# A GRU scan on one core: one token block's input product moved between the one-product warm-up steps

## The chip, the cores and the metric

One core of one Trainium2 chip. The metric is the device time of one execution in microseconds (us); the kernel before took 2601.79 us in the median of three runs.

## What is computed

```python
def cell(h, x):                       # h [4, 1024], weights [1024, 3072]
    gi = x @ W_ih + b_ih
    gh = h @ W_hh + b_hh
    r = sigmoid(i_r + h_r); z = sigmoid(i_z + h_z)
    n = tanh(i_n + r * h_n)
    return (1 - z) * n + z * h
...
hs = scan(cell, cond, x over 1024 positions)      # x [4, 1024, 1024] f32
y = x + ffn(hs)    # layer norm, routing to one of 64 spline tiles, spline of 16 features
```

## The kernel before

**Work and layout.** The 4 sequences of 1024 positions are cut into 16 chunks of 64 positions, so 64 columns are scanned at once, in two sets (SETS) of 32. A chunk's start state isn't known, so the scan first warms up: from a zero state it runs the last 44 positions (20 to 63) of every chunk. 24 of these steps (WARM_HEADS) use one product, the f16 high part of the state by the high part of the weights; 20 (WARM_FULL) use three products (high by high, high by low, low by high). The end states become the next chunks' start states. Then the pass runs all 64 positions: 44 with three products, 20 as differences from sums stored in the warm-up. The pass also routes tokens, and a last part evaluates the splines. The one-product steps are called **heads** below, and one step of one set a half-step.

**Input product** (`input_product`, from L75). gi = x W_ih + b for all 4096 tokens in 8 blocks (NBLK) of 512 tokens, ordered by position, so block 0 holds positions 0 to 7 of all chunks and block 7 positions 56 to 63. A block is 24 PSUM banks (6 blocks of 512 weight columns, CBLOCKS, by 4 token tiles, TB). A bank takes 24 matmuls: 8 slices k of the inner dimension by three products of the split halves (L290 to L292). ACT makes the high halves (L184, L188), DVE the low ones (L229, L234). DVE evicts a bank, adding the bias (`evict`, L242), and ACT's queue stores it to `gi_scratch` in DRAM (`store_gi`). SP loads a block's x ahead (`load_x`, L126), the pieces of the weights (`load_w`, L123) and copies x rows (`begin_rows`, L131). In the last block W_hh is loaded and split into the room of W_ih, each column block after its last use.

**Recurrence** (`recurrence`, from L338). The split W_hh stays in SBUF. For a set, `pe_products` (L478 to L483) issues 8 x 4 matmuls of 512 columns into the set's r, z bank and 8 x 4 of 256 columns into its n bank; the four of a slice go to four column quarters of PE (128x32 weights). `dve_step` (L692) and `act_step` (L574) then run in turn: sums (L703, L706), sigmoids (L582, L583), r times n (L710), plus gi (L714), tanh (L587), new state (L719, L724), transpose (L728), and the f16 state for the next product (ACT, L592). PE, ACT and DVE each take set a, then set b, in the order of the code; sets alternate. In the heads the loop is

```python
with pe.Fori(0, WARM_HEADS // 2) as it:
    for u in range(2):
        pe_run(pe, it, u, 1, HEADS)
```

and alike on ACT and DVE. SP loads the gi record of a set two steps ahead: it waits until the slot's n part is used (`gi_used`, L1031) and issues four DMAs of 32 partitions by 3 KB (`load_gi`, L1024). These are 16 increments each on `gi_loaded`, for which DVE waits. Before the heads SP loads the spline tables and h0 (L1095, L1097), and POOL splits the tables. After the full steps SP issues, in this order, the records of the pass's first positions, the stores of sums and states, and the shifted start states (`shift_starts`, L1081), for which DVE waits before it sets the pass's start (L859). PE transposes routing hits between products in the pass (`pe_turn`, L521), and in the difference steps adds stored sums by 128x128 matmuls (L501) ahead of a product.

Of the kernel before, what the change touches and what calls it, by code (L numbers as in the profile page):

```python
# [73 lines left out]

def input_product(nc, ctx, t, W_ih, W_hh, b_ih, b_hh, xT, gi_dram, slopes, gamma, beta, gamma_t, beta_t,  # L75
                  out_scale, sign_dram, x_rows, hs_dram):
# [10 lines left out]
    x_hi = sb("x_hi", [P, 2, KB, BW], F16)  # L87
    x_lo = sb("x_lo", [P, 2, KB, BW], F16)
    out_stage = sb("out_stage", [P, TB, CW])
    bias_row = sb("bias_row", [P, QUARTERS, QW])  # L90
# [18 lines left out]
    sign_stored, rows_loaded, rows_ready = sem("sign_stored"), sem("rows_loaded"), sem("rows_ready")  # L109

# [4 lines left out]
    with nc.Block() as block:  # L115

        @block.sync
        def _(sp):
# [6 lines left out]
            def load_x(n, k):  # L125
                sp.dma_start(xstage[:, k:k + KX], xT.rearrange("(k p) n -> p k n", p=P)[:, k:k + KX, bass.ds(n * BW, BW)])\  # L126
                  .then_inc(x_loaded[k // KX], 16)
# [40 lines left out]
            with sp.Fori(1, NBLK - 1) as n:  # L168
                sp.wait_ge(x_hi_ready, n * XPARTS + XPARTS)
                sp.sem_inc(wait_carrier, 1)  # L170
                sp.wait_ge(x_lo_ready, n * XPARTS + XPARTS)
                sp.sem_inc(wait_carrier, 1)
                for k in range(0, KB, KX):
                    load_x(n + 1, k)
                begin_rows(n * 5 - 3, 5)

# [9 lines left out]
        def split_x_hi(act, n, buf, k):  # L186
            act.wait_ge(x_loaded[k // KX], n * 16 + 16)
            nc.scalar.activation(x_hi[:, buf, k:k + KX], xstage[:, k:k + KX], ACT.Copy, scale=S_SCALE).then_inc(x_hi_ready, 1)  # L188

        def store_gi(act, n, e):  # L190
            cb, tb = divmod(e, TB)
            act.wait_ge(acc_free, n * ACCS + (BANKS + e + 1))
            act.dma_start(gi_dram[bass.ds(n * BW + tb * P, P), cb * CW:(cb + 1) * CW], out_stage[:, tb]).then_inc(gi_stored[tb], 16)

        @block.scalar
        def _(act):
# [12 lines left out]
            with act.Fori(1, NBLK - 1, 2) as n:  # L209
                for u in range(2):  # L210
                    for e in range(ACCS):
                        if e == 8:
                            act.wait_ge(acc_ready, (n + u) * ACCS)
                            act.sem_inc(wait_carrier, 1)
                            for k in range(0, KB, KX):
                                split_x_hi(act, n + u + 1, u, k)
                        store_gi(act, n + u, e)
            for cb in range(CBLOCKS):
                for tb in range(TB):
                    store_gi(act, NBLK - 1, cb * TB + tb)  # L220
                act.wait_ge(acc_ready, (NBLK - 1) * ACCS + (cb + 1) * TB)
                for kp in range(XPARTS):
                    split_w_hi(act, PIECES + cb * XPARTS + kp, cb * XPARTS + kp)
            for b in range(TB):
                act.wait_ge(gi_stored[b], 16 * NBLK * CBLOCKS)
# [6 lines left out]
        def split_x_lo(dve, n, buf, k):  # L232
            dve.wait_ge(x_hi_ready, n * XPARTS + (k // KX + 1))
            nc.vector.scalar_tensor_tensor(out=x_lo[:, buf, k:k + KX], in0=xstage[:, k:k + KX], scalar=S_SCALE,  # L234
                                           in1=x_hi[:, buf, k:k + KX], op0=ALU.mult, op1=ALU.subtract).then_inc(x_lo_ready, 1)
# [11 lines left out]
        def _(dve):  # L247
# [19 lines left out]
            with dve.Fori(1, NBLK - 1, 2) as n:  # L267
                for u in range(2):
                    for e in range(ACCS):
                        if 12 <= e < 12 + XPARTS:  # L270
                            split_x_lo(dve, n + u + 1, u, (e - 12) * KX)
                        evict(dve, n + u, e, False)
            for cb in range(CBLOCKS):
                for tb in range(TB):
                    evict(dve, NBLK - 1, cb * TB + tb, False)
# [8 lines left out]
        def _(pe):  # L284
            def products(u, e, ks):
                cb, tb = divmod(e, TB)
                for k in ks:
                    hi, lo = x_hi[:, u, k, tb * P:(tb + 1) * P], x_lo[:, u, k, tb * P:(tb + 1) * P]
# [23 lines left out]
            with pe.Fori(1, NBLK - 1, 2) as n:  # L312
# [4 lines left out]
            pe.wait_ge(x_lo_ready, NBLK * XPARTS)  # L317
            for e in range(ACCS):
                whole(NBLK - 1, 1, e)
# [18 lines left out]
def recurrence(nc, ctx, t, h0, gi_dram, sums_dram, states_dram, hs_dram, x_rows, y_rows, tables):  # L338
# [16 lines left out]
    w_hi, w_lo, h, hi, flag = t["w_hi"], t["w_lo"], t["h"], t["hi"], t["flag"]  # L355
    lo = sb("lo", [P, SETS, JB, COLS], F16)
# [4 lines left out]
    saved = sb("saved", [P, SETS, 2, QW], F16)  # L361
# [11 lines left out]
    h_start = sb("h_start", [P, SETS, QF])  # L373
    next_start = sb("next_start", [P, SETS, QF])
# [8 lines left out]
    h_tok = sb("h_tok", [P, D])  # L383
    xhat = sb("xhat", [P, D])
    signed = sb("signed", [P, D])
    signs = sb("signs", [P, D], BF16)
# [4 lines left out]
    scores = sb("scores", [P, NT])  # L391
    tkeys = sb("tkeys", [P, NT])
    csums = sb("csums", [P, CLUSTERS])
    keys = sb("keys", [P, NT])
    best = sb("best", [P, 1])
    hit = sb("hit", [P, NT])
    hit_ids = sb("hit_ids", [P, NT])
    tile_id = sb("tile_id", [P, 1])
    row_f = sb("row_f", [P, 1])
    pick_now = sb("pick_now", [P, SLICE])  # L400
    row_now = sb("row_now", [P, 1], I32)
    affine_left = sb("affine_left", [NT, 2, 2 * SLICE])
    normal = sb("normal", [P, ENDS_MOST, SLICE])
    tok_ends = sb("tok_ends", [P, 2, ENDS_MOST])
    miss = sb("miss", [P, ENDS_MOST, NT])

    ends_hit = saved[:].rearrange("p s a f -> p (s a f)").bitcast(F32)[:, 0:ENDS_MOST * NT].rearrange("p (i t) -> p i t", t=NT)
    batch_ends = sb("batch_ends", [P, 2, NT])

    curves, *curves_left = (a[0:NT, 0:2 * SLICE * GRID] for a in (xhat, signed, h_tok))  # L410
    rstd, shift, hits, hits_t = t["rstd"], t["shift"], t["hits"], t["hits_t"]
# [5 lines left out]
    affine = pb("affine", [P, TILES, 2 * SLICE])  # L417

# [20 lines left out]
    wait_carrier = sem("wait_carrier2")  # L439
# [1001 lines left out]
```

## Time and profile before

| | |
|---|---|
| three runs | 2601.41, 2601.79, 2604.37 us |
| the profiled execution | 2604.53 us, span 2602.7 us |
| mean granted TensorE clock | 0.964 |
| input product, first to last matmul | 11.2 to 1019.2 us |
| heads, first matmul to first full step | 1032.20 to 1246.75 us |
| busy share of the span: PE, DVE, ACT, POOL | 90%, 50%, 26%, 7% |

The span is from the first to the last instruction; the execution's own time is 1.8 us more. Busy times are of one profiled execution. A matmul's record runs on while the next has begun, so a PE that is busy all the time isn't one at its peak; starts of successive matmuls tell the rate. The granted clock is a share of 2.4 GHz: 1.00 or 0.50 (1.2 GHz), in a stretch their mean.

### The profile page before, as it was taken

Reading aid. Unit: us, or ns where it says so; the run is one execution under the profiler, and the core shown is the slowest. Engines: PE = TensorE matmul, PEld = TensorE weight load, DVE = VectorE, ACT = ScalarE, POOL = GpSimd, SP = SyncE. Lnnn points to the kernel's source line nnn. Section 1 sums busy time; section 2 is a strip of 40 time slices with the busy share of each in tenths; the row PEclk is TensorE's granted clock in tenths of the full one; section 3 lists DMA queues with packets and bytes.
Section 4 is the critical chain, followed back from the end, with each engine's and each line's share of the span. In section 5 each row is a group of like instructions: output and inputs, shape, how many; then the busy total and the mean of one; then the engine's idle time right before and its main releaser. Section 6 shows DMA issues by size and latency. Waiting matters only on the chain. (4 is left out here: it accounts for less than half of the span.)

```text
span 2602.7 us, 83556 instructions
## 1 busy us (share of the span) xinstructions
PE 2354.0 (90%) x35300; PEld 1289.6 (50%) x35300; DVE 1291.3 (50%) x2644; ACT 668.9 (26%) x1340; POOL 189.1 (7%) x376
## 2 busy tenths in 40 slices
PE   7999999999999997666999998999999999977734
PEld 3444444444444443333666664666666666633311
DVE  4321121211111133777666664666666666877765
ACT  2200000000000012444333332333333333355520
POOL 0000000000000000000000000011111111121217
PEclk9999999999999998999999998999999999999955
DMA  6543131313131144333344443444444444477722
GB/s 213 182 150 125 53 121 54 121 53 122 51 140 53 49 150 141 95 88 87 120 138 129 136 138 86 122 114 113 114 120 122 113 114 120 122 225 222 221 50 4
DMA packets 160438, 305.21 MB, mean 117 GB/s; under 512 B 26832, under 2 KB 76416, under 8 KB 159296
## 3 DMA queue, kind: packets, MB, share of 16 engines
q1 hardware_dynamic: 122448, 236.06, 28.8%
q10 hardware_dynamic: 27648, 50.34, 5.2%
q0 software_dynamic: 10240, 17.31, 4.5%
q8 instruction: 80, 1.31, 0.2%
q14 instruction: 22, 0.18, 0.0%
HBM read 209.54 MB, written 144.18 MB: 136 GB/s over the span
## 5 line engine op out<-in xcount | busy, mean ns | idle before, releaser
L290 PE MATMUL acc<-w_hi,x_hi 128*128 128x512 f16 x1536 | 584.0, 380 | 19.7 <-DVE x_lo L234 11.2
L291 PE MATMUL acc<-w_hi,x_lo 128*128 128x512 f16 x1536 | 583.9, 380 | 0.0
L292 PE MATMUL acc<-w_lo,x_hi 128*128 128x512 f16 x1536 | 583.7, 380 | 0.0
L483 PE MATMUL rz_bank<-w_hi,hi 128*32 128x512 f16 x6912 | 427.7, 391 | 150.7 <-ACT hi L592 69.5
L242 DVE SCALAR_TENSOR_TENSOR out_stage<-acc,bias_row 128x512 f32<-128x512 f32 x192 | 132.3, 691 | 719.7 <-PE acc L292 719.7
L483 PEld LDWEIGHTS rz_bank<-w_hi,hi 128*32 128x32 f16 x6912 | 177.8, 98 | 326.9 <-ACT hi L592 81.5
L290 PEld LDWEIGHTS acc<-w_hi,x_hi 128*128 128x128 f16 x1536 | 150.6, 98 | 203.0 <-issue 16.0
L483 PE MATMUL rz_bank<-w_lo,hi 128*32 128x512 f16 x4096 | 243.1, 379 | 0.0
L483 PE MATMUL rz_bank<-w_hi,lo 128*32 128x512 f16 x4096 | 243.1, 379 | 0.0
L292 PEld LDWEIGHTS acc<-w_lo,x_hi 128*128 128x128 f16 x1536 | 150.6, 98 | 182.5 <-issue 2.2
L291 PEld LDWEIGHTS acc<-w_hi,x_lo 128*128 128x128 f16 x1536 | 150.6, 98 | 181.7 <-issue 1.7
L582 ACT ACTIVATE rz<-sums 128x512 f32<-128x512 f32 x176 | 110.9, 630 | 495.5 <-DVE sums L703 495.4
L483 PE MATMUL n_bank<-w_hi,hi 128*32 128x256 f16 x6912 | 232.9, 278 | 0.0
L703 DVE SCALAR_TENSOR_TENSOR sums<-rz_bank,gi 128x512 f32<-128x512 f32 x176 | 120.4, 684 | 205.2 <-PE rz_bank L483 204.6
L483 PEld LDWEIGHTS n_bank<-w_hi,hi 128*32 128x32 f16 x6912 | 189.7, 99 | 56.7 <-issue 6.8
L188 ACT ACTIVATE x_hi<-xstage 128x1024 f16<-128x1024 f32 x32 | 31.8, 1046 | 667.3 <-DVE out_stage L242 662.3
L483 PEld LDWEIGHTS rz_bank<-w_hi,lo 128*32 128x32 f16 x4096 | 109.0, 97 | 84.7
L483 PEld LDWEIGHTS rz_bank<-w_lo,hi 128*32 128x32 f16 x4096 | 109.0, 97 | 84.7 <-issue 0.2
L483 PE MATMUL n_bank<-w_hi,lo 128*32 128x256 f16 x4096 | 133.9, 273 | 0.0
L483 PE MATMUL n_bank<-w_lo,hi 128*32 128x256 f16 x4096 | 133.9, 273 | 0.0
L587 ACT ACTIVATE n_act<-n_sum 128x256 f32<-128x256 f32 x216 | 90.2, 418 | 166.6 <-DVE n_sum L714 166.0
L483 PEld LDWEIGHTS n_bank<-w_lo,hi 128*32 128x32 f16 x4096 | 109.0, 97 | 30.1
(158 smaller groups left out, 2013.8 us busy)
## 6 DMA issues: line engine op xcount, KB each, us to landing
gi<-gi_scratch SPq DMA_DIRECT2D x704, 96.0 KB
gi_scratch<-out_stage ACTq DMA_DIRECT2D x192, 256.0 KB, 2.1
gi<-sums_scratch SPq DMA_DIRECT2D x40, 512.0 KB
xstage<-in_xT SPq DMA_DIRECT2D x32, 512.0 KB, 6.0
y<-in_x_rows SPq DMA_DIRECT2D x32, 512.0 KB, 4.4
hs_scratch<-h SPq DMA_DIRECT2D x128, 128.0 KB
h_tok<-hs_scratch SPq DMA_DIRECT2D x32, 512.0 KB, 3.9
y<-hs_scratch POOLq DMA_DIRECT2D x32, 512.0 KB, 7.8
```

What stands on the lines that cost most here:

```text
L188: nc.scalar.activation(x_hi[:, buf, k:k + KX], xstage[:, k:k + KX], ACT.Copy, scale=S_SCALE).then_inc(x_hi_ready, 1)
L242: nc.vector.scalar_tensor_tensor(out=out_stage[:, tb], in0=acc[e % BANKS][:], scalar=UNSCALE, in1=bias_row[:].rearrange("p q f -> p (q f)" ...
L290: nc.tensor.matmul(acc[e % BANKS][:], hi, wh, start=k == 0, stop=False)
L291: nc.tensor.matmul(acc[e % BANKS][:], lo, wh, start=False, stop=False)
L292: last = nc.tensor.matmul(acc[e % BANKS][:], hi, wl, start=False, stop=k == KB - 1)
L483: last = nc.tensor.matmul(bank[q * COLS:(q + 1) * COLS, 0:b - a], state[:, s, j], w[:, j, q * QW + a:q * QW + b], start=first and j == 0, ...
L582: nc.scalar.activation(rz[:, s], sums[:, s, 0:RZ], ACT.Sigmoid).then_inc(rz_ready[s], 1)
L587: nc.scalar.activation(n_act[:, s], n_sum[:, s], ACT.Tanh).then_inc(n_ready[s], 1)
L703: nc.vector.scalar_tensor_tensor(out=sums[:, s, 0:RZ], in0=rz_bank[s][:], scalar=UNSCALE, in1=gi[:, s, u, 0:RZ], op0=ALU.mult, op1=ALU.add ...
```

## The change

- The input product makes blocks 1 to 7 only (EARLY_BLOCKS = 7). Block 0's x is loaded and split last, into `x_keep`, and is kept. After the first block's weight splits SP stores both halves of W_ih to DRAM (`late_w`, 16 DMAs).
- In the heads PE does 12 matmuls of 128x512 after each half-step's product (`pe_late`): slice k of one column block for the four token tiles, into the four PSUM banks that only later parts use. 48 half-steps are 6 column blocks by 8 slices. The weights come from `late_w` through a ring of four slots of 256 KB. After each eighth slice DVE evicts the four banks, two within its step and two behind it, and SP stores them to `gi_scratch`.
- A gi record is loaded by one DMA instead of four, in all stages that load them.
- The tables and h0 are loaded after the heads. PE and ACT wait after the heads for the last evictions, ACT before the pass for the row splits.
- Many tiles of the recurrence lie in the room of the kept x, the bias and the late results, with the same shapes.

The diff, cut to what the steps speak of:

```diff
             begin_rows(0, 2)
-            with sp.Fori(1, NBLK - 1) as n:
+            sp.wait_ge(w_hi_ready, PIECES)
+            sp.wait_ge(w_lo_ready, PIECES)
+            for k in range(KB):
+                for part, w in enumerate((w_hi, w_lo)):
+                    sp.dma_start(late_w[k, :, :, part],
+                                 w[:, k].rearrange("p (c f) -> p c f", f=CW)).then_inc(late_w_stored, 16)
+            with sp.Fori(1, EARLY_BLOCKS - 1) as n:
                 sp.wait_ge(x_hi_ready, n * XPARTS + XPARTS)
...
+                    evict(dve, EARLY_BLOCKS - 1, cb * TB + tb, False)
+                    if cb == 0:
+                        split_x_lo(dve, EARLY_BLOCKS, 1, tb * KX)
...
 
+        def pe_late(pe, cb, k):
+            pe.wait_ge(late_loaded[k % RING], cb * (KB // RING * 16) + (k // RING * 16 + 16))
+            pe.sem_inc(wait_carrier, 1)
+            wh, wl = late_ring[:, k % RING, 0], late_ring[:, k % RING, 1]
+            for tb in range(TB):
+                if k == 0:
+                    pe.wait_ge(late_free[tb], cb + 1)
+                    pe.sem_inc(wait_carrier, 1)
+                x_hi, x_lo = (x_late[:, part, k, tb * P:(tb + 1) * P] for part in range(2))
+                nc.tensor.matmul(late_acc[tb], x_hi, wh, start=k == 0, stop=False)
+                nc.tensor.matmul(late_acc[tb], x_lo, wh, start=False, stop=False)
+                last = nc.tensor.matmul(late_acc[tb], x_hi, wl, start=False, stop=k == KB - 1)
+                if k == KB - 1:
+                    last.then_inc(late_done, 1)
+            if k < KB - 1:
+                last.then_inc(late_used, 1)
         def pe_turn(pe, T):
...
             pe.sem_inc(hit_turned, 1)
-            with pe.Fori(0, WARM_HEADS // 2) as it:
-                for u in range(2):
-                    pe_run(pe, it, u, 1, HEADS)
+            def heads(cb):
+                for i in range(LATE_STEPS):
+                    pe_run(pe, cb * 2 + i // 2, i % 2, 1, HEADS,
+                           after=tuple((lambda k=i * SETS + s: pe_late(pe, cb, k)) for s in range(SETS)))
+            with pe.Fori(0, CBLOCKS) as cb:
+                heads(cb)
+            for tb in range(TB):
+                pe.wait_ge(late_free[tb], CBLOCKS + 1)
             with pe.Fori(WARM_HEADS // 2, WARM // 2) as it:
...
                 turns = p + 1
+                if first:
+                    act.wait_ge(rows_split, 5)
                 for s in range(SETS):
...
 
-        def dve_step(dve, it, u, s, seeds, mode=FULL):
+        def dve_late(dve, cb, tb):
+            dve.wait_ge(late_done, cb * TB + (tb + 1))
+            dve.sem_inc(wait_carrier, 1)
+            dve.wait_ge(late_stored[tb], cb * 16 + 16)
+            dve.sem_inc(wait_carrier, 1)
+            nc.vector.scalar_tensor_tensor(out=late_out[:, tb], in0=late_acc[tb], scalar=UNSCALE, in1=bias_room[:, bass.ds(cb * CW, CW)],
+                                           op0=ALU.mult, op1=ALU.add).then_inc(late_free[tb], 1)
+        def dve_step(dve, it, u, s, seeds, mode=FULL, after_sums=None, after_old=None):
             n = steps_to(it, u)
...
                                                op0=ALU.mult, op1=ALU.add).then_inc(hn_ready[s], 1)
+                if after_sums:
+                    after_sums()
                 dve.wait_ge(rz_ready[s], n)
...
             nc.vector.tensor_tensor(z_old[:, s], rz[:, s, QF:RZ], h_old, ALU.mult).then_inc(z_old_ready[s], 1)
+            if after_old:
+                after_old()
...
                     dve.sem_inc(h_stored[s][u], 16)
-            with dve.Fori(0, WARM_HEADS // 2) as it:
-                for u in range(2):
+            for tb in range(TB):
+                dve.sem_inc(late_free[tb], 1)
+                dve.sem_inc(late_stored[tb], 16)
+            with dve.Fori(0, CBLOCKS) as cb:
+                for i in range(LATE_STEPS):
                     for s in range(SETS):
-                        dve_step(dve, it, u, s, 1, HEADS)
+                        if i * SETS + s < KB - 1:
+                            dve_step(dve, cb * 2 + i // 2, i % 2, s, 1, HEADS)
+                        else:
+                            dve_step(dve, cb * 2 + i // 2, i % 2, s, 1, HEADS, lambda: dve_late(dve, cb, 0), lambda: dve_late(dve, cb, 1))
+                            dve_late(dve, cb, 2)
+                            dve_late(dve, cb, 3)
             for s in range(SETS):
...
 
-        def gi_rows(pos, s, q, a, b):
-            return gi_dram[bass.ds(pos * POS + s * COLS, COLS), q * QW + a:q * QW + b]
+        def load_late(sp, cb, k):
+            sp.dma_start(late_ring[:, k % RING], late_w[k, :, bass.ds(cb, 1)].rearrange("p o a f -> p (o a) f"))\
+              .then_inc(late_loaded[k % RING], 16)
 
         def load_gi(sp, pos, s, u):
-            for q in range(QUARTERS):
-                sp.dma_start(gi[q * COLS:(q + 1) * COLS, s, u, 0:QW], gi_rows(pos, s, q, 0, QW)).then_inc(gi_loaded[s][u], 16)
+            sp.dma_start(gi[:, s, u, 0:QW], gi_dram[bass.ds(pos * POS + s * COLS, COLS)].rearrange("c (q f) -> q c f", q=QUARTERS))\
+              .then_inc(gi_loaded[s][u], 64)
 
...
                     load_gi(sp, LEN - WARM + u, s, u)
+            for k in range(RING):
+                load_late(sp, 0, k)
+            def heads(cb, last):
+                for i in range(LATE_STEPS):
+                    for s in range(SETS):
+                        it, u, k = cb * 2 + i // 2, i % 2, i * SETS + s
+                        gi_used(sp, it, s, u)
+                        load_gi(sp, it * 2 + (LEN - WARM + 2 + u), s, u)
+                        if k < KB - RING or not last:
+                            if k < KB - 1:
+                                sp.wait_ge(late_used, cb * (KB - 1) + (k + 1))
+                            else:
+                                sp.wait_ge(late_done, cb * TB + TB)
+                            sp.sem_inc(wait_carrier, 1)
+                            load_late(sp, cb + (k + RING) // KB, (k + RING) % KB)
+                for tb in range(TB):
+                    sp.wait_ge(late_free[tb], cb + 2)
+                    sp.sem_inc(wait_carrier, 1)
+                    sp.dma_start(gi_dram[tb * P:(tb + 1) * P, bass.ds(cb * CW, CW)], late_out[:, tb]).then_inc(late_stored[tb], 16)
+            with sp.Fori(0, CBLOCKS - 1) as cb:
+                heads(cb, False)
+            heads(CBLOCKS - 1, True)
             sp.dma_start(curves, tables[:]).then_inc(curves_loaded, 16)
             for q in range(QUARTERS):
                 sp.dma_start(next_start[q * COLS:q * COLS + BATCH, 0], h0[q]).then_inc(h0_loaded, 16)
-            with sp.Fori(0, WARM_HEADS // 2) as it:
-                for u in range(2):
-                    for s in range(SETS):
-                        gi_used(sp, it, s, u)
-                        load_gi(sp, it * 2 + (LEN - WARM + 2 + u), s, u)
             for s in range(SETS):
...
             def one_pass(p, first):
+                if first:
+                    for tb in range(TB):
+                        sp.wait_ge(late_stored[tb], (CBLOCKS + 1) * 16)
                 for u in range(2):
```

## Rows read from the trace of the kernel before

**Rows 1.** The page: busy time of the whole span, and one matmul group.

```profile
PE 2354.0 (90%) x35300; PEld 1289.6 (50%) x35300; DVE 1291.3 (50%) x2644; ACT 668.9 (26%) x1340; POOL 189.1 (7%) x376
...
L290 PE MATMUL acc<-w_hi,x_hi 128*128 128x512 f16 x1536 | 584.0, 380 | 19.7 <-DVE x_lo L234 11.2
```

**Rows 2.** Busy time by stretch; columns: stretch, then length and busy us (x instructions).

```profile
500.00:550.00 50.00, 50.00 (x234) 22.63 (x232) 6.23 (x9) 0.00 (x0) 0.00 (x0) 1.00 0.14 53
1100.00:1150.00 50.00, 31.22 (x716) 18.14 (x720) 38.38 (x90) 24.11 (x49) 0.00 (x0) 1.00 0.32 90
1300.00:1350.00 50.00, 50.00 (x1237) 32.85 (x1228) 31.44 (x65) 17.88 (x39) 0.00 (x0) 1.00 0.44 142
```

**Rows 3.** Timeline of DVE and PE in one half-step of the heads.

```profile
1099.77 0.65 DVE L703 SCALAR_TENSOR_TENSOR sums<-rz_bank,gi 128x512 f32<-128x512 f32 x1
...
1103.91 0.65 DVE L703 SCALAR_TENSOR_TENSOR sums<-rz_bank,gi 128x512 f32<-128x512 f32 x1
...
1104.49 0.40 PE L483 MATMUL rz_bank<-w_hi,hi 128*32 128x512 f16 x4 [1.36 <-ACT hi L592]
```

**Rows 4.** Timeline of PE: first product of the heads, first product of the full steps.

```profile
1032.20 3.60 PE L483 MATMUL rz_bank<-w_hi,hi 128*32 128x512 f16 x32 [12.99 <-ACTq L636]
...
1246.75 1.91 PE L483 MATMUL rz_bank<-w_hi,hi 128*32 128x512 f16 x32 [1.36 <-ACT hi L592]
```

**Rows 5.** Busy time by stretch: start of the heads, and a later 5 us.

```profile
1035.00:1040.00 5.00, 5.00 (x104) 3.08 (x96) 2.73 (x6) 1.35 (x3) 0.00 (x0) 0.73 0.58 171
...
1150.00:1155.00 5.00, 5.00 (x88) 2.75 (x80) 4.01 (x10) 2.21 (x6) 0.00 (x0) 0.66 0.31 83
```

**Rows 6.** Timeline of DVE, last bank evictions of block 0; start us, duration us.

```profile
141.52 0.69 DVE L242 SCALAR_TENSOR_TENSOR out_stage<-acc,bias_row 128x512 f32<-128x512 f32 x1 [3.36 <-PE acc L292]
...
146.70 0.69 DVE L242 SCALAR_TENSOR_TENSOR out_stage<-acc,bias_row 128x512 f32<-128x512 f32 x1 [3.36 <-PE acc L292]
```

**Rows 7.** Timeline of PE in a full step.

```profile
1582.84 1.89 PE L483 MATMUL rz_bank<-w_hi,hi 128*32 128x512 f16 x32
1584.57 1.04 PE L483 MATMUL n_bank<-w_hi,hi 128*32 128x256 f16 x32
1585.44 1.89 PE L483 MATMUL rz_bank<-w_lo,hi 128*32 128x512 f16 x32
```

**Rows 8.** Timeline of PE where column quarters meet a wider tile.

```profile
1730.88 1.05 PE L483 MATMUL n_bank<-w_hi,lo 128*32 128x256 f16 x32
1731.86 0.30 PE L521 MATMUL hit_bank<-ident,hit 128*64 128x128 f32 x1
1732.08 1.91 PE L483 MATMUL rz_bank<-w_hi,hi 128*32 128x512 f16 x32
...
2358.01 1.05 PE L483 MATMUL n_bank<-w_hi,hi 128*32 128x256 f16 x32
2358.99 0.60 PE L501 MATMUL rz_bank<-gi,ident_sum 128*128 128x512 f16 x2
```

**Rows 9.** The page's DMA queues: packets, MB, share of 16 engines' span.

```profile
q1 hardware_dynamic: 122448, 236.06, 28.8%
```

**Rows 10.** Timeline of SP's DMA issues and of DVE at the pass's start.

```profile
1093.97 14.23 SPq L1024 DMA_DIRECT2D gi<-gi_scratch  x16
...
1564.78 1.76 SPq L1024 DMA_DIRECT2D gi<-gi_scratch  x4
...
1567.13 3.38 SPq L1081 DMA_DIRECT2D next_start<-h  x4
...
1571.84 0.29 DVE L859 COPY h_start<-next_start 128x256 f32<-128x256 f32 x1 [7.47 <-DMA next_start<-h]
...
2356.09 0.36 SPq L1049 DMA_DIRECT2D gi<-sums_scratch  x1
```

**Rows 11.** SP's issue of block 2's x; an issue group (KB each, us to landing).

```profile
143.60 2.09 SPq L126 DMA_DIRECT2D xstage<-in_xT  x4
...
hs_scratch<-in_x_rows SPq DMA_DIRECT2D x6, 2560.0 KB, 14.3
```

More of the change, by code:

```diff
@@ L86, in input_product @@
     xstage = sb("xstage", [P, KB, BW])
-    x_hi = sb("x_hi", [P, 2, KB, BW], F16)
-    x_lo = sb("x_lo", [P, 2, KB, BW], F16)
+    x_even = sb("x_even", [P, 2, KB, BW], F16)
+    x_hi, x_lo = ([x_even[:, part], t["x_keep"][:, part]] for part in range(2))
     out_stage = sb("out_stage", [P, TB, CW])
-    bias_row = sb("bias_row", [P, QUARTERS, QW])
+    bias_row = t["bias_row"]
     bias_h = sb("bias_h", [P, QUARTERS, RZ])
@@ L175, in _ @@
                 begin_rows(n * 5 - 3, 5)
+            sp.wait_ge(x_hi_ready, EARLY_BLOCKS * XPARTS)
+            sp.wait_ge(x_lo_ready, EARLY_BLOCKS * XPARTS)
+            for k in range(0, KB, KX):
+                load_x(EARLY_BLOCKS, k)
+            begin_rows(27, 5)
             for m in range(PIECES):
@@ L208, in _, with act_block @@
                 store_gi(act, 0, e)
-            with act.Fori(1, NBLK - 1, 2) as n:
-                for u in range(2):
[L211 to L217, printed above, removed]
+            def act_block(n, buf):
+                for e in range(ACCS):
+                    if e == 8:
+                        act.wait_ge(acc_ready, n * ACCS)
+                        act.sem_inc(wait_carrier, 1)
+                        for k in range(0, KB, KX):
+                            split_x_hi(act, n + 1, buf, k)
+                    store_gi(act, n, e)
+            with act.Fori(1, EARLY_BLOCKS - 2, 2) as n:
+                for u in range(2):
+                    act_block(n + u, u)
+            act_block(EARLY_BLOCKS - 2, 0)
+            act.wait_ge(acc_ready, (EARLY_BLOCKS - 1) * ACCS)
+            for k in range(0, KB, KX):
+                split_x_hi(act, EARLY_BLOCKS, 1, k)
+            act.wait_ge(late_w_stored, 16 * 2 * KB)
             for cb in range(CBLOCKS):
                 for tb in range(TB):
-                    store_gi(act, NBLK - 1, cb * TB + tb)
-                act.wait_ge(acc_ready, (NBLK - 1) * ACCS + (cb + 1) * TB)
+                    store_gi(act, EARLY_BLOCKS - 1, cb * TB + tb)
+                act.wait_ge(acc_ready, (EARLY_BLOCKS - 1) * ACCS + (cb + 1) * TB)
                 for kp in range(XPARTS):
@@ L311, in _ @@
                 whole(0, 0, e)
[L312 removed]
+            with pe.Fori(1, EARLY_BLOCKS - 2, 2) as n:
                 for u in range(2):
@@ L316, in _ @@
                         whole(n + u, 1 - u, e)
-            pe.wait_ge(x_lo_ready, NBLK * XPARTS)
-            for e in range(ACCS):
-                whole(NBLK - 1, 1, e)
+            for u in range(2):
+                pe.wait_ge(x_lo_ready, (EARLY_BLOCKS - 1 + u) * XPARTS)
+                for e in range(ACCS):
+                    whole(EARLY_BLOCKS - 2 + u, 1 - u, e)
 TILE_UNIT, CLUSTER_UNIT = 64, 272
@@ L439, in recurrence @@
     wait_carrier = sem("wait_carrier2")
+    late_loaded = [sem(f"late_loaded{i}") for i in range(RING)]
+    late_free, late_stored = ([sem(f"{n}{i}") for i in range(TB)] for n in ("late_free", "late_stored"))
+    late_used, late_done = sem("late_used"), sem("late_done")
     row_known, hit_kept, picked, pick_kept = (sem(n) for n in ("row_known", "hit_kept", "picked", "pick_kept"))
@@ L1113, in one_pass @@
             def one_pass(p, first):
+                if first:
+                    for tb in range(TB):
+                        sp.wait_ge(late_stored[tb], (CBLOCKS + 1) * 16)
                 for u in range(2):
```

101 lines of the change are left out of this document (58 added, 43 removed).

## The prediction

> **What bounds the kernel now.** I read the page first: PE is busy 90% of the span [rows 1]. That share mixes stages, so the next view was busy time by stretch [rows 2]. In the input product (500 to 550 us) PE is busy the whole time, DVE 6.2 us and the DMA engines 14%: PE alone sets the time. In the warm-up steps of one product (1100 to 1150 us; called heads below) PE is busy 31.2 of 50 us, DVE 38.4 and the DMA share is 0.32. In the full steps (1300 to 1350 us) PE is full again. So work in the first stage costs its whole PE time, and the heads have PE time to spare: the change carries work from the one to the other.
>
> The timeline of the heads says what they wait for [rows 3]. A half-step (one step of one set) is 32 matmuls of 512 columns and 32 of 256, four at a time on column quarters. DVE begins the sums of one set at 1099.77 and of the other at 1103.91: 4.14 us a half-step. From the sums to the first matmul that uses their state is 1104.49 - 1099.77 = 4.72 us, all of it DVE and ACT in turn. DVE works through one set's chain, waits for ACT included, before it takes the other's, so DVE's order bounds this stage. 48 half-steps at 4.14 us are 198.7 us, yet the stage runs from 1032.20 to 1246.75 [rows 4], 214.55 us; part of the rest is short spells at TensorE's lower level, such as a mean granted clock of 0.66 at 1150 to 1155 us [rows 5].
>
> **What is removed.** One of eight token blocks leaves the input product. A bank is evicted each 146.70 - 141.52 = 5.18 us [rows 6], which is 24 matmuls of 0.216 us; a block is 24 banks: **-124.3 us**, all of it on the path that sets the end.
>
> **What the heads get.** Each half-step gets 12 matmuls of the same shape: 12 x 0.216 = 2.59 us. Its own product, when nothing is waited for, takes 1585.44 - 1582.84 = 2.60 us [rows 7]. Together 5.19 us, over DVE's 4.14, so PE becomes the bound. Does the chain hide? From the start of a set's product its sums begin at most 2.6 us later, when the whole product is done, and the state is back 4.72 us after that: 7.3 us. The set's turn on PE comes again after two half-steps, 10.4 us or more. It hides with 3 us to spare. In every eighth half-step DVE also evicts four banks at 0.69 us [rows 6], 2.8 us; the spare 1 us of each half-step takes it back within three, and PE uses the four banks again only after the next product, 2.6 us on. I cost these evictions at nothing; if that cover failed, they would add at most 5 x 2.8 = 14 us.
>
> **The seam between the two kinds of matmul** appears twice in each half-step and nowhere in the heads of before. The nearest rows [rows 8]: from the start of a 256-column part to the next instruction is 0.87 us within column quarters (1584.57 to 1585.44, [rows 7]), but 2358.99 - 2358.01 = 0.98 us when a 128-wide matmul follows, and again 0.98 us before the transpose at 1731.86: 0.11 us to leave the quarters. The transpose and the way back take 0.22 us, its own work included, so going back costs between nothing and 0.2 us. Bounds for both seams: 0 (were the weights loaded ahead) to 0.35 us, which also has room for the two extra queue instructions of each late step. I take 0.15, near the 0.11 that rows show. The Trainium skill, "TensorEngine Tiling (Array Packing)", Key Properties, says that changing the tiling mode drains the engine; the 0.98 against 0.87 us agrees in sign, and what a full drain at both seams would make of it is the first rival.
>
> Heads after: 48 x (2.60 + 2.59 + 0.15) = 256.3 us. To it come three single costs. The stage begins after 12.99 us of idle PE [rows 4] at the lower of the two levels; the mean of 0.73 over 1035 to 1040 [rows 5] puts the rise near 1037.7, so 5.5 us go at half speed, which costs a stage that PE bounds 2.7 us. From then on PE has no idle, as in the product and the full steps, where the clock is 1.00 [rows 2], so I expect no further fall. Second, the first late weights are behind 1.5 MB of first records in SP's queue; at 315 GB/s (queue q1 moved 236.06 MB in 28.8% of 2602.7 us of all engines [rows 9]), 5.6 us with the first weights' 0.25 MB, and some 1.5 us for issue and landing, they land near 1039, 1.6 us after PE has done its first product; bounds 0 and 5. Third, at the end PE waits for all four late banks to be evicted: DVE's last half-step (4.14 us and two evictions in it) starts some 3.2 us before PE's end (0.87 of the 256-column part and 2.59 of the late group, less a hand-over), and two more evictions follow, so PE stands about 4.0 us; bounds 0 and 7. Sum 256.3 + 2.7 + 1.6 + 4.0 = 264.6 against 214.55: **+50.1 us**.
>
> **Queues.** SP issues per head half-step four loads now, 14.23 us for 16 [rows 10], 3.6 of 4.14 us. A single load of 128 partitions takes 0.36 us to issue (at 2356.09, [rows 10]). After the change SP issues one such load and one of 256 KB, under 1 us of 5.3, with waits that are met before its turn (the bank's use, at the end of each late step; the next record is needed two steps on). The late load is asked for three half-steps, 16 us, ahead; a DMA of ten times its bytes lands in 14.3 us [rows 11]. Bytes per half-step: 384 + 256 KB, and 1 MB of results each eighth, about 145 GB/s, what the full steps carry already at a share of 0.44 [rows 2]. Nothing. Behind the four waits for the evictions in SP's queue stand the next record loads, due 10 us later: nothing. At the start of the pass the four record loads take 1.76 us to issue, ahead of the state's four DMAs of 3.38 us, for which DVE waits until 1571.84 and PE behind it [rows 10]. One load instead of four: **-1.4 us** (bounds 0 and -1.4). Elsewhere in the full steps PE covers SP.
>
> **The store of the split weights**, 12.6 MB in 1 KB pieces from about 132 us on, stands in SP's queue ahead of the x load that is issued at 143.60 [rows 11]. The DRAM-to-DRAM row of 2.6 MB in 14.3 us gives 183 GB/s [rows 11], and so 69 us: the x lands near 215 us. Block 1 starts near 146 us [rows 6], ACT holds its ninth store for this x, DVE's thirteenth eviction waits for that store, and PE would stop at its 21st bank, 146 + 20 x 5.18 = 250 us. Cover 35 us; cost nothing. If the store went at half that rate, PE would stand some 35 us: the upper bound of a case that I give little. The last block also splits the kept x: four pieces of twice an eviction's size, so about 1.4 us each by its 0.69, on ACT and DVE between evictions 5.18 us apart: hidden. The table load and POOL's splits move behind the heads, where twenty full steps cover them.
>
> **Sum** against the profiled execution: 2604.53 - 124.3 + 50.1 - 1.4 = 2528.9 us. It was 2.7 us above the median of 2601.79, so the forecast is **2526 us**.
>
> **Rivals.** (1) Both seams drain the array. A matmul is in the records for 0.38 us [rows 1] and the next starts after 0.216, so 0.16 us is in flight; two seams make 0.33 instead of 0.15 us: +8.6, 2535 us. For: 0.11 is already most of one drain. Against: the return at the transpose leaves little room. (2) The chain isn't hidden after all: a late group stands in front of each set's product and the half-step is 4.14 + 2.59 = 6.73 us; 323 us, 2593 us. Against: the two sets alternate on PE, and 6.7 us is well under 10.4. (3) The x load behind the store comes late, up to 35 us: to 2561 us. Against: the 35 us of cover at a cautious rate. (4) **Slower**: the clock. The heads are the stage in which it falls now [rows 5], and a stage bound by PE pays for each fall, where now DVE covers most of it. With the lower level all through, a half-step is 5.19 us longer: +249, 2775 us. It decides from the point at which the heads last 214.55 + 124.3 + 1.4 = 340 us, 7 us a half-step, which is half of the stage at the lower level. For: short waits of PE at each ring load would bring such falls. Against: the clock is 1.00 wherever PE has no idle. (5) Seams for nothing and evictions and starts hidden: 2514 us. That the work isn't moved can't be: the block is gone from one list of instructions and stands in another.
>
> **Chances.** Forecast 0.62, (1) 0.20, (5) 0.05, (2) 0.04, (3) 0.04, (4) 0.03, anything unseen 0.02. The range 2513 to 2550 goes down to all single costs at nothing and up to a seam of 0.35 us (+9.6), the upper bounds of start and end (+6.4) and half of the evictions uncovered (+7). A measurement of this kernel can tell 0.2%, 5 us, from no change. Faster by more 0.95, within 0.01, slower 0.04.
>
> **What would show it.** PE's stage of the input product ends near 895 us rather than 1019. In the heads PE is busy without idle at clock 1.00, half-steps start 5.3 us apart, DVE's idle is ended by PE's bank rather than by ACT, and the half-step after each eighth isn't longer. Seams: 0.98 or more from the last 256-column part to the first late matmul. A single wait of some 4 us for the late banks ahead of the first full step. Wrong, if PE waits in the heads for a DMA or for ACT's state, if clocks under 1.00 show there beyond the first 6 us, if block 1 or 2 of the product has a gap, or if the first full step starts later than 265 us after the first head.

## The result, and the profile after

The changed kernel takes 2581.77 us in the median (2579.61 to 2582.41) beside 2601.6 us for the kernel before on the same chip: a ratio of 0.9916, interval 0.9904 to 0.9929. It is faster by 0.8%, 20 us, where 76 us were forecast, and lies outside the range of 2513 to 2550 us.

The places at which the stages meet, in the timeline of PE of the changed kernel: the first product of the heads, the first late matmul, the first full product, the first product of the pass (before: [rows 4, 10]). In brackets stand the idle time of PE ahead of it and what ended it.

```profile
906.96 3.56 PE L526 MATMUL rz_bank<-w_hi,hi 128*32 128x512 f16 x32 [13.09 <-ACTq L703]
...
928.64 0.59 PE L571 MATMUL hit_bank<-late_ring,x_keep 128*128 128x512 f16 x1 [17.24 <-DMA late_ring<-late_w_scratch]
...
1192.15 1.91 PE L526 MATMUL rz_bank<-w_hi,hi 128*32 128x512 f16 x32 [3.79 <-DVE late_out L768]
...
1549.92 3.61 PE L526 MATMUL rz_bank<-w_hi,hi 128*32 128x512 f16 x32 [31.18 <-ACT hi L724]
```

The differences of such starts are the lengths of the stages, in us (the pass of before starts at 1573.19; its own row is in its timeline):

```profile
1573.19 3.60 PE L483 MATMUL rz_bank<-w_hi,hi 128*32 128x512 f16 x32 [14.25 <-ACT hi L653]
```

| stage | before | after | forecast change | measured change |
|---|---|---|---|---|
| up to the heads | 1032.20 | 906.96 | -124.3 | -125.2 |
| heads | 214.55 | 285.19 | +50.1 | +70.6 |
| full steps, to the pass's first product | 326.44 | 357.77 | -1.4 | +31.3 |
| from there to the end of the span | 1029.5 | 1029.7 | 0 | +0.2 |

So the block left as forecast. Against the forecast 53 us are missing in these traces, 20 in the heads and 33 in a stage that I had counted as untouched but for the 1.4. (By the medians it is 56: the profiled execution of before lay 2.7 us above its median, the one of after lay at its median.) The waits name the places: 17.24 us for the first late weights, 31.18 us of idle PE ahead of the pass instead of 14.25, and a full warm-up that is no longer full. Busy time by stretch, after (columns as in [rows 2]):

```profile
1000.00:1050.00 50.00, 50.00 (x724) 25.37 (x720) 34.78 (x77) 17.51 (x38) 0.00 (x0) 1.00 0.44 145
...
1400.00:1450.00 50.00, 47.61 (x1148) 30.29 (x1152) 27.82 (x59) 16.69 (x36) 0.00 (x0) 1.00 0.35 119
```

From 150 to 200 us, while the split weights go to DRAM at a DMA share of 0.96, PE is busy all the 50 us: covered. The steady heads are as forecast, PE without idle at clock 1.00. At 1400 to 1450 us, in full warm-up steps, PE does 1148 matmuls where such steps held 1237 in [rows 2]. The waits of those steps (1200 to 1520 us), ACT's and SP's own:

```profile
ACT warm_state L669 <- DMA states_scratch<-warm_state: 118.3, 31, 4.5
...
SPq L1124 <- DMA sums_scratch<-gi: 193.6, 36, 6.0
```

Before the change neither stood there: ACT's idle was ended by DVE's sums, SP's by DVE's split of the sums. Both new waits are for small stores that SP queues behind a record's load. What the records do to the DMA engines shows where little else runs. The DMA view of 912 to 928 us, after, in 40 slices of 0.4 us, and of 1035 to 1041 us, before (0.15 us):

```profile
DMA  2222222479788997876962222222222222222222
GB/s 115 100 92 92 115 100 92 113 218 361 143 177 243 241 179 212 223 113 141 335 213 69 92 100 115 92 100 100 108 100 92 100 108 100 100 95 100 92 102 102
```

```profile
DMA  6769289488749610101002565979069489846855
GB/s 143 307 185 348 62 225 294 164 185 205 307 103 287 246 21 0 20 0 21 0 20 82 184 246 185 287 246 287 0 266 287 143 307 266 144 184 246 266 184 185
```

A record loaded by one DMA moves at about 100 GB/s with a steady share of the engines: from 921 to 926 us it is 0.26, at 101 GB/s, and four of 16 engines would be 0.25. The hump in the middle fits the four late weights, which SP issues from 909.31 to 918.37 us. It is over near 920 us, and PE still waits for the first of them until 928.64 us. Loaded by four DMAs a record has up to 0.9 of the engines. The theory for the runs: **the one DMA runs on 4 of the 16 engines**, because its source pattern begins with a dimension of 4 (quarters, 32 columns, 768 numbers), so its bytes line up at 4 engines (at their "rings", in the expectations below) and hold up what SP queues behind them. The Trainium skill says this in "DMA: Bandwidth & Descriptors", section "Why a DMA increments its semaphore by 16 and not by 1": a DMA issued by SP or ACT is split over the largest number of engines, up to 16, that divides the slowest dimension of both of its patterns. The 0.26 agrees with four engines. The rival: the late work crowds the queue, however the records are loaded.

### The profile page after: what moved, and what is told of

Its sections match the earlier page's. It is cut to its first block and busy times, and to the rows that moved or that the text cites. A ratio compares the mean times of both kernels' runs of the same rounds, so it can differ in the third digit from the quotient of the medians.

```text
span 2579.6 us, 82162 instructions
## 1 busy us (share of the span) xinstructions
PE 2352.5 (91%) x35300; PEld 1284.4 (50%) x35300; DVE 1290.6 (50%) x2644; ACT 663.1 (26%) x1334; POOL 188.5 (7%) x376
## 5 line engine op out<-in xcount | busy, mean ns | idle before, releaser
L526 PE MATMUL rz_bank<-w_hi,hi 128*32 128x512 f16 x6912 | 420.7, 386 | 113.6 <-DVE hi L817 54.8
L270 DVE SCALAR_TENSOR_TENSOR out_stage<-acc,bias_row 128x512 f32<-128x512 f32 x168 | 115.6, 691 | 609.6 <-PE acc L326 609.6
L324 PE MATMUL acc<-w_hi,x_even 128*128 128x512 f16 x768 | 293.6, 382 | 17.8 <-DVE x_even L262 11.2
L325 PE MATMUL acc<-w_hi,x_even 128*128 128x512 f16 x768 | 293.6, 382 | 0.0
L326 PE MATMUL acc<-w_lo,x_even 128*128 128x512 f16 x768 | 293.3, 382 | 0.0
L324 PE MATMUL acc<-w_hi,x_keep 128*128 128x512 f16 x576 | 218.6, 379 | 0.1
L325 PE MATMUL acc<-w_hi,x_keep 128*128 128x512 f16 x576 | 218.6, 379 | 0.0
L326 PE MATMUL acc<-w_lo,x_keep 128*128 128x512 f16 x576 | 218.6, 379 | 0.0
L324 PEld LDWEIGHTS acc<-w_hi,x_even 128*128 128x128 f16 x768 | 75.4, 98 | 110.1 <-issue 13.6
L526 PEld LDWEIGHTS n_bank<-w_hi,lo 128*32 128x32 f16 x4096 | 109.6, 97 | 29.5
```

The costliest lines, as they stand in the source:

```text
L270: nc.vector.scalar_tensor_tensor(out=out_stage[:, tb], in0=acc[e % BANKS][:], scalar=UNSCALE, in1=bias_row[:].rearrange("p q f -> p (q f)" ...
L324: nc.tensor.matmul(acc[e % BANKS][:], hi, wh, start=k == 0, stop=False)
L325: nc.tensor.matmul(acc[e % BANKS][:], lo, wh, start=False, stop=False)
L326: last = nc.tensor.matmul(acc[e % BANKS][:], hi, wl, start=False, stop=k == KB - 1)
L526: last = nc.tensor.matmul(bank[q * COLS:(q + 1) * COLS, 0:b - a], state[:, s, j], w[:, j, q * QW + a:q * QW + b], start=first and j == 0, ...
```

## The experiments

All ratios are to the kernel before on the same chip. Lengths of stages are read from starts as above.

### e1_four_loads: the records by four DMAs again

```diff
-            sp.dma_start(gi[:, s, u, 0:QW], gi_dram[bass.ds(pos * POS + s * COLS, COLS)].rearrange("c (q f) -> q c f", q=QUARTERS))\
-              .then_inc(gi_loaded[s][u], 64)
+            for q in range(QUARTERS):
+                sp.dma_start(gi[q * COLS:(q + 1) * COLS, s, u, 0:QW],
+                             gi_dram[bass.ds(pos * POS + s * COLS, COLS), q * QW:(q + 1) * QW]).then_inc(gi_loaded[s][u], 16)
```

> The changed kernel with the gi record loaded by four DMAs of 32 partitions again; all else stays. Theory (the one DMA, whose source begins with a dimension of 4, runs on 4 of the 16 DMA engines): the idle before the first late matmul falls from 17.2 us to under 5, the full warm-up half-step from about 8.3 to 7.8 us, the idle of PE at the start of the pass from 31.2 to about 14 us; the time is 2527 us, within 8. Rival (late weights, their results and the records crowd the queue, however the records are loaded): the time stays within 10 us of 2582.

Measured: 2538.61 us, ratio 0.9758 (0.9741 to 0.9774), 43 us under the changed kernel. Heads 273.5 us, full steps to the pass 328.5. Its PE timeline, where the heads, the full steps and the pass begin:

```profile
905.86 3.60 PE L526 MATMUL rz_bank<-w_hi,hi 128*32 128x512 f16 x32 [13.32 <-ACTq L703]
...
1179.39 2.60 PE L526 MATMUL rz_bank<-w_hi,hi 128*32 128x512 f16 x32 [3.79 <-DVE late_out L768]
...
1507.93 3.61 PE L526 MATMUL rz_bank<-w_hi,hi 128*32 128x512 f16 x32 [14.68 <-ACT hi L724]
```

The idle ahead of the pass is 14.68 us again, the full half-steps are 7.8 us again, and the wait for the first late weights is 5.1 us (of 17.2). A late weight lands 4.0 us after its issue in the median of the first four; with the one DMA it took 14.4. The rival's 2582 is ruled out: the late work with its ring and stores is still all there. 11.7 us come back in the heads, 29.2 in the full steps and the pass's start. The time is 11.6 us over the expected 2527, just outside the 8 us given; e6 below takes 11.9 us away again.

### e2_before_merged: the kernel before with the one DMA, and no late work

```diff
-            for q in range(QUARTERS):
-                sp.dma_start(gi[q * COLS:(q + 1) * COLS, s, u, 0:QW], gi_rows(pos, s, q, 0, QW)).then_inc(gi_loaded[s][u], 16)
+            sp.dma_start(gi[:, s, u, 0:QW], gi_dram[bass.ds(pos * POS + s * COLS, COLS)].rearrange("c (q f) -> q c f", q=QUARTERS))\
+              .then_inc(gi_loaded[s][u], 64)
```

> The kernel before with nothing changed but the one DMA a record. Theory: a record takes some 5.1 us on 4 engines, more than the 4.14 us of a half-step, so the heads are bound by it: 48 x 5.1 = 245 us against 214.6, +30; the full warm-up steps lose 0.4 us a half-step, +16; the pass starts some 17 us later; about 2665 us, between 2630 and 2690. Rival (crowding by the late work): there is none here, so 2602 us within 5.

Measured: 2639.32 us, ratio 1.0141 (1.0124 to 1.0158). The one DMA alone costs 37 us without any late work, mostly in the same places: full steps to the pass 359.5 us instead of 326.4, with 31.17 us of idle ahead of the pass:

```profile
1608.79 3.23 PE L483 MATMUL rz_bank<-w_hi,hi 128*32 128x512 f16 x32 [31.17 <-ACT hi L653]
```

My number for its heads was wrong: +4.5 us, not +30. I had taken 5.1 us a record from the start of the changed kernel, where four records and the first late weights stand in line. At 102 GB/s a record of 393 KB takes 3.9 us, just under the 4.14 us of a half-step.

### e5_two_loads: two DMAs a record, each with an outer dimension of 2

```diff
+            for a in range(0, QUARTERS, 2):
+                sp.dma_start(gi[a * COLS:(a + 2) * COLS, s, u, 0:QW],
+                             gi_dram[bass.ds(pos * POS + s * COLS, COLS), a * QW:(a + 2) * QW].rearrange("c (q f) -> q c f", q=2))\
+                  .then_inc(gi_loaded[s][u], 32)
```

> The changed kernel with two DMAs a record, each of 64 partitions with a source that begins with a dimension of 2. Theory: 2 engines each, the same two for both, so a record takes some 10.2 us, over every half-step of the heads (5.4), the full warm-up (7.8) and the pass's 88 full half-steps (7.8): +230, +96 and +210 us over e1, about 3060 us, at least 2900. Rival (it is the length of one DMA, so halves are better than the whole): at most 2582 us.

Measured in a single execution: 3107.2 us. From the DMA view of its 912 to 928 us (the last number of the second line is the share of the 16 engines):

```profile
DMA packets 271, 0.80 MB, mean 50 GB/s; under 512 B 9, under 2 KB 9, under 8 KB 271
...
q1 hardware_dynamic: 271, 0.80, 12.9%
```

50 GB/s, half of the 102, and a share of 0.129, half of the 0.26, for half of the outer dimension. Cutting the DMA in two halved the rate of a record, so the length of one DMA isn't what counts. The figures fit 4 and 2 engines (0.25 and 0.125 of 16) at 25 GB/s each, and the two halves on the same two. The records of the trace don't name engines, so the count is inferred from rates and shares; the rule of the Trainium skill agrees at both points. The total came near the expected 3060 us partly by luck: over e1 the heads grew by 172 us (230 expected), the full steps with the pass's start by 183 (96 expected) and the rest by 214 (210 expected).

### e9_state_before_load and e10_shift_first: what stands behind the record in SP's queue

With the one DMA kept, only SP's order is changed. e9, in the loop of full warm-up steps:

```diff
                         store_sums(sp, it, s, u)
+                        store_state(sp, it, s, u)
                         gi_used(sp, it, s, u, True)
                         load_gi(sp, it * 2 + (LEN - WARM + 2 + u), s, u)
-                        store_state(sp, it, s, u)
```

> The changed kernel with the one DMA a record kept, and in the loop of full warm-up steps SP stores the set's state ahead of the next record's load, not behind it. Theory (a record on 4 of the 16 rings holds up what SP queues behind it there; the state's store lands late and ACT, which waits for it, stands 126 us in these steps): the full steps' half-step falls from 8.2 to 7.8 us, 14 us less than the changed kernel, 2568 us, and the heads stay at 285 us. Rival (the store of the record's kept part, which waits for the record itself, is what holds SP): under 4 us less.

Measured: 2568.96 us, ratio 0.9873 (0.9856 to 0.9889), 13 us under the changed kernel. ACT's wait for the state's store falls from 118.3 us to 10.3, and without the idle ahead of the pass the full steps take 313.9 us, where they took 326.6 in the changed kernel and 312.2 before. SP's own wait for the store of the record's kept part is still 151.3 us in e9, so within these steps that one was long but covered. Heads and start of the pass are untouched (285.2 us; 29.84 us of idle).

At the start of the pass it isn't covered. There the changed kernel's timeline shows SP's issue of the shifted start states and DVE's first use of them:

```profile
1541.04 3.34 SPq L1176 DMA_DIRECT2D x_keep<-h  x4
...
1548.51 0.29 DVE L953 COPY x_keep<-x_keep 128x256 f32<-128x256 f32 x1 [16.27 <-DMA x_keep<-h]
```

PE's idle begins at 1518.74 us, so SP issues the shift 22.3 us later; before the change it was 8.2 us ([rows 10], idle from 1558.94). That is 14.1 of the 16.9 us of added idle. In these 30 us SP waits three times, 17.9 us in all, for the store of a record's kept part before it may load the next record, and the shift stands behind. Only 2.8 us are the shift's own landing: 4.1 us after the end of its issue instead of 1.3. e10 adds to e9:

```diff
+                if first:
+                    for u in range(2):
+                        for s in range(SETS):
+                            store_sums(sp, WARM // 2 - 1, s, u)
+                            store_state(sp, WARM // 2 - 1, s, u)
+                    shift_starts(sp, WARM // 2 - 1)
                 for u in range(2):
                     for s in range(SETS):
-                        if first:
-                            store_sums(sp, WARM // 2 - 1, s, u)
                         gi_used(sp, pair_of(p, -1), s, u, first)
                         load_gi(sp, u, s, u)
-                        if first:
-                            store_state(sp, WARM // 2 - 1, s, u)
-                if first:
-                    shift_starts(sp, WARM // 2 - 1)
```

> As e9_state_before_load, the one DMA a record kept, and at the start of the pass SP stores the last sums and states and shifts the start states ahead of the four record loads of the pass's first positions. Theory (on 4 of 16 rings the records ahead of the shifted states are what makes PE stand 29.8 us there instead of 14.3): PE's idle falls to 13 to 16 us, the time to about 2554 us. Rival (the wait is for the last full step's own stores): it stays over 25 us, 2565 us or more.

Measured: 2551.62 us, ratio 0.9808 (0.9792 to 0.9824).

```profile
1516.80 3.23 PE L526 MATMUL rz_bank<-w_hi,hi 128*32 128x512 f16 x32 [12.30 <-ACT hi L724]
```

12.3 us of idle, just below the 13 to 16 expected and under the 14.25 of before, and 326.2 us from the first full product to the pass, what it was before the change: all of the 31.3 us lost there are back, at the slow records' own speed. In these stages the records themselves weren't late; what SP had queued behind them was, its own waits included. In the heads no run keeps the one DMA and puts the late weights ahead of it.

### e6_start_and_wait, e4_group_after_a, e7_group_evict_early, e8_all: the rest, and a better order

These start from e1. e6:

```diff
             for u in range(2):
                 for s in range(SETS):
+                    load_late(sp, 0, u * SETS + s)
                     load_gi(sp, LEN - WARM + u, s, u)
-            for k in range(RING):
-                load_late(sp, 0, k)
...
-            for tb in range(TB):
-                pe.wait_ge(late_free[tb], CBLOCKS + 1)
             with pe.Fori(WARM_HEADS // 2, WARM // 2) as it:
                 for u in range(2):
                     pe_run(pe, it, u, 1)
+            for tb in range(TB):
+                pe.wait_ge(late_free[tb], CBLOCKS + 1)
```

> As e1_four_loads, with two waits of PE shortened: at the start of the heads SP asks for each late weight ahead of the record it stood behind, and PE waits for the last late banks ahead of the pass, not ahead of the full steps. Theory (of e1's 273.5 us of heads 5.1 are the wait for the first late weights, 2.4 the second spell at the lower level that this wait brings, 3.8 the wait at the end, and 1.7 us of the full steps the spell that follows it): 8 to 13 us less than e1, 2526 to 2531 us; no spell at the lower level after the first. Rival (the first records are what the stage waits for, so their delay takes the gain back): 4 us less or nothing.

Measured: 2526.69 us, ratio 0.9708 (0.9692 to 0.9724), 11.9 us under e1. Heads 261.0 us, full steps 326.8. In e1 the clock had risen to the upper level near 911 us and fell again during the wait of 5.1 us; in e6, without the wait, it stays up after the first spell. Busy time by stretch of e1:

```profile
911.00:916.00 5.00, 0.06 (x4) 0.00 (x0) 2.91 (x7) 1.11 (x3) 0.00 (x0) 0.82 0.81 235
916.00:921.00 5.00, 4.79 (x12) 1.65 (x12) 0.00 (x0) 0.00 (x0) 0.00 (x0) 0.50 0.59 183
```

e4 puts both late groups of a step behind set a's product:

```diff
-                           after=tuple((lambda k=i * SETS + s: pe_late(pe, cb, k)) for s in range(SETS)))
+                           after=((lambda i=i: (pe_late(pe, cb, i * SETS), pe_late(pe, cb, i * SETS + 1))), None))
```

> As e1_four_loads, but both late groups of a step stand behind set a's product, 24 matmuls together, and none behind set b's. One pair of seams a step instead of two. If a pair of seams costs the 0.22 us that the trace of the changed kernel shows, 24 x 0.22 = 5.3 us less than e1, and some 2.5 us less at the end of the heads, where the late banks are done one product earlier: about 2519 us. Rival (PE's order must alternate, or set b's chain is not hidden behind 7.8 us): the heads grow longer than e1's by over 10 us.

Measured: 2542.48 us, ratio 0.9770 (0.9753 to 0.9786): 4 us slower than e1, not 8 faster. Its steps are 10.60 us where e1's are 10.82, so the saved pair of seams does give 0.22 us; but the first step of each later column block takes 11.82, and 5.85 us of wait stand at the end. The waits of PE in the heads, 930 to 1180 us, name it:

```profile
PE affine L571 <- DVE late_out L768: 5.3, 5, 1.1
```

Five times PE wants the banks before DVE has evicted them. e7 moves the evictions into the time in which DVE waits for set b's product:

```diff
-                            dve_step(dve, cb * 2 + i // 2, i % 2, s, 1, HEADS, lambda: dve_late(dve, cb, 0), lambda: dve_late(dve, cb, 1))
-                            dve_late(dve, cb, 2)
-                            dve_late(dve, cb, 3)
+                            for tb in range(TB):
+                                dve_late(dve, cb, tb)
+                            dve_step(dve, cb * 2 + i // 2, i % 2, s, 1, HEADS)
```

> As e4_group_after_a, with the four evictions of every eighth half-step ahead of set b's step on DVE, while PE does set b's product, not in and behind it. Theory (e4's steps of 10.60 us show the saved pair of seams, 0.22 us a step, but the steps of 11.82 and the end of 5.85 us show PE waiting for banks that DVE evicts too late): all steps 10.6 us, no wait at the end; 5.3 + 3.8 + 1.7 = 10.8 us less than e1, about 2528 us. Rival (the steps of 11.82 us come from set b's chain, late behind two groups): the long steps stay, and the time is within 3 us of e4's 2542.

Measured: 2529.30 us, ratio 0.9717 (0.9700 to 0.9733). No wait for a late bank is left, and the heads take 263.8 us. e8 is e7 with e6's edits:

> e7_group_evict_early with e6's order at the start and PE's wait ahead of the pass. Theory: e7's 10.8 us and e6's 5 to 7.5 us at the start add up: 16 to 18 us less than e1, 2521 to 2523 us. Rival (with two groups ahead of set b's first product two late weights must be there, so the start gains nothing): within 2 us of e7.

Measured: 2521.07 us, ratio 0.9686 (0.9670 to 0.9702), heads 255.8 us. Last, e8 with e10's order at the pass:

> The same reordering of the pass's start in e8_all, where records are loaded by four DMAs. Theory: the four record loads ahead take 1.76 us to issue and little to land, so PE's idle of 14.6 us falls by 1 to 3 us: 2518 to 2520 us. Rival (the first records then come late for the pass's first sums): the idle or the first step grows, 2521 us or more.

Measured: 2518.81 us, ratio 0.9679 (0.9663 to 0.9695), idle ahead of the pass 12.31 us instead of 14.64. The medians of e8 and e11 are 2.3 us apart in different sets of runs, less than the 0.2% that can be told; the idle in the profile is what changed. This is the best version: 3.2% under the kernel before, four times the gain of the change as made.

## Why the prediction was wrong, step by step

- **The block removed**: right, 125.2 us against 124.3.
- **Steady heads**: right in mechanism. PE became the bound, the chain of DVE and ACT and the evictions hid, and a half-step takes 5.41 us against 5.34. The **seam** was mis-sized: 0.22 us a pair, not 0.15; e4's shorter steps confirm it. 48 x 0.07 = 3.4 us. The timeline of the changed kernel shows both halves: 0.98 us from the start of the 256-column part to the late matmul, 0.11 more than within quarters, and 0.31 us from the last late matmul to the product where a late one follows a late one after 0.216:

```profile
1006.08 1.05 PE L526 MATMUL n_bank<-w_hi,hi 128*32 128x256 f16 x32
1007.06 0.39 PE L571 MATMUL hit_bank<-late_ring,x_keep 128*128 128x512 f16 x1
...
1009.45 0.38 PE L573 MATMUL affine<-late_ring,x_keep 128*128 128x512 f16 x1
1009.76 1.91 PE L526 MATMUL rz_bank<-w_hi,hi 128*32 128x512 f16 x32
```

  So the two seams are about 0.1 us each, less than the 0.33 a pair that my first rival assumed. Whether this time is a drain no run shows.
- **Queues, the step that failed.** I wrote of the one DMA: "A single load of 128 partitions takes 0.36 us to issue", and then "Nothing". I priced the issue, from a DMA whose both sides have 128 rows, and put the landing of the record, and of what follows it, at nothing. This one's source has an outer dimension of 4. It moved 102 GB/s at a quarter of the engines' time, and behind it in SP's queue stood the first late weights, the kept part's and the state's stores and the shifted starts. The terms, after against e1: +11.7 us in the heads, +12.7 in the full steps and +16.5 at the pass's start, where I had -1.4. e1 and e2 show that it is this DMA, e9 and e10 that in the full steps and at the pass's start it acts through what is queued behind it. e5 shows that the rate goes with the outer dimension, and the shares of 0.26 and 0.129 fit 4 and 2 engines, a count that is inferred. For the heads the way through the queue is argued from the trace alone.
- **The first late weights**: 1.6 us forecast, 17.2 measured, of which 12 are the one DMA's. The 5.1 us of e1 are my rate: I took 315 GB/s, an average of busy engines over the whole span; the four loads move about 200 at this place. SP needs 7.3 us to issue the first 16 of them and the first late weight follows at 913.02 us, so issue may set this rate; no run parts the two. This wait also brought a second spell at the lower level, 2.4 us. I had said that short waits at ring loads would bring such falls, and gave that only to the rival that ends slower. My argument against it, a clock of 1.00 wherever PE has no idle, isn't what [rows 5] say: PE is busy all of both stretches of 5 us, at 0.73 and 0.66. Idle of PE had come shortly before both.
- **The end of the heads**: 3.79 us against 4.0, right. In e1 a spell at the lower level follows it, 1.7 us in the full steps, which I had left out; the changed kernel's trace has the same wait and no such spell.
- **The pass's start**: the issue did get shorter, from the last record's load to the shift 1.18 us (1539.86 to 1541.04) instead of 2.35, but SP came to it 14 us later, so nothing of it was left. With four loads a record, e11 gives 2.3 us by putting the shift ahead of them.
- **The store of the split weights** hid, as forecast.

With the records loaded as before, e1's 2538.6 lies in the range, 12.6 us over the forecast. In its trace the heads and full steps are 12.4 us longer than forecast: the seams (3.4), the start (5.7, the second spell included; the end gives back 0.2), the spell behind the end (1.7) and 1.8 us at the pass, where 1.4 were forecast as a gain and 0.4 were lost. The input product is 2.0 us shorter than forecast and the part behind 0.7, so the profiled execution (2538.48 us) is 9.6 over the sum of 2528.9. The other 3 us of the 12.6 are mostly the 2.7 that I had taken off, because before's profiled execution lay above its median; e1's lies at its median.

## What to carry to other kernels

When several DMAs are folded into one, price its landing and not only its issue: look at the outermost dimension of both sides. With 4 rows there a DMA moved 102 GB/s here and with 2 rows 50, where DMAs of 32 rows moved some 200; by the rule of the Trainium skill given above, only a multiple of 16 on both sides gets all 16 engines. What stands behind such a DMA in the queue pays, in stages that the change seems not to touch. And where late-needed loads and stores share a queue with small ones that an engine waits for, the small ones go first; that order alone gave back 30 us here.

## What the runs showed that was not expected

- A DMA with an outer dimension of 4 moves 102 GB/s and one with 2 about 50 GB/s, the four DMAs of 32 rows some 200.
- In the heads of before, steps take 8.29 and 9.44 us in turn, in e2 too: one half-step in four takes 5.30 us, not 4.14. ACT's timeline names what stands in it, once in each turn of the loop of two steps:

```profile
1108.60 1.28 ACT L582 ACT_TABLE_LOAD   x1
```

  ACT loads its function table again ahead of the sigmoid, in DVE's and ACT's chain, which bounds this stage, and DVE waits 1.37 us for that sigmoid, not 0.36. The first of the 12 loads stands ahead of the first sums; the other 11 make some 11 x 1.15 = 12.7 of the 15.9 us between 198.7 and 214.55 that I had put down in part to the clock. In the full steps ACT's timeline shows no such load, and every half-step takes 7.80 us. In the changed kernel's heads there are five behind the first, one for each later turn of its longer loop, and they hide behind PE: its half-steps stay at 5.41 us. Why the load comes once a turn, and taking it out, were not tried.
